# A spare copy with a drain on VectorE, 15 times in each half of a lookup, gram and MLP kernel

## The reference

```python
e = jnp.stack([tbl_f[ids[:, f]] for f in range(27)], axis=1)      # 2048 x 27 x 128
x = jnp.einsum('bfd,bgd->bfg', e, e).reshape(B, 27 * 27)[:, TRIL_IDX]
h = jnp.concatenate([r_bottom_mlp_out, x, r_bottom_mlp_out], axis=1)
h = jnp.maximum(h @ W_top1 + b_top1, 0.0)       # 607 -> 512
h = jnp.maximum(h @ W_top2 + b_top2, 0.0)       # 512 -> 256
y = h @ W_top3                                  # 256 -> 1
```

## Time and profile before

| what | value |
|---|---|
| timed runs, median of 3 | 412.73 us (412.5 to 413.49) |
| profiled execution, span from the first to the last instruction | 563.8 us |
| the profiled execution's own time | not recorded apart from its span |
| TensorE matmul, busy | 395.0 us (70%), 3669 instructions |
| VectorE, busy | 231.8 us (41%), 430 |
| ScalarE, busy | 156.7 us (28%), 337 |
| GpSimd, busy | 292.0 us (52%), 284 |
| mean granted TensorE clock | 0.845 |
| DMA traffic | 40.50 MB, mean 72 GB/s |

### The profile page before, as it was taken

How to read it: one execution, slowest core, us unless ns; L and a number is a source line. 1 busy time by engine, 2 the same in 40 slices (tenths; PEclk the granted TensorE clock), 3 DMA queues, 4 the chain that set the end, 5 groups by cost and what they waited for, 6 DMA issues and landing times.

```text
span 563.8 us, 9147 instructions
## 1 busy us (share of the span) xinstructions
PE 395.0 (70%) x3669; PEld 336.8 (60%) x3669; DVE 231.8 (41%) x430; ACT 156.7 (28%) x337; POOL 292.0 (52%) x284
## 2 busy tenths in 40 slices
PE   1620868397979578688939587797979490924987
PEld 1520756285868467576737376676857390823977
DVE  3530667073836143373617052472716050422430
ACT  3200543021424142324115042322215041401433
POOL 6776007656574747374735737373746656172010
PEclk9975898688989979699969879697979785885999
DMA  8761272122331312041411212140413111030000
GB/s 212 193 170 47 79 185 70 48 84 66 93 86 29 99 35 74 23 118 34 145 28 62 76 33 72 24 117 24 131 37 75 48 53 51 6 95 19 16 8 9
DMA packets 20737, 40.50 MB, mean 72 GB/s; under 512 B 7128, under 2 KB 11428, under 8 KB 20696
## 3 DMA queue, kind: packets, MB, share of 16 engines
q1 hardware_dynamic: 11674, 21.64, 14.1%
q0 software_dynamic: 8960, 18.22, 12.8%
q10 hardware_dynamic: 62, 0.06, 0.1%
HBM read 36.81 MB, written 0.01 MB: 65 GB/s over the span
## 4 chain that ended last, share of the span: by engine, by line
PE 51%; issue 18%; another core or an unknown queue 11%; DVE 8%; DVEq 3%; ACT 3%; DMA 3%; SPq 1%; ACTq 0%
PE col_bank L687 17%; PE gram_bank L723 15%; PE mlp_bank L778 6%; PE mlp_bank L746 6%; DVE mask L583 4%; PE col_bank L706 4%; DVEq L590 3%; PE mlp_bank L742 2%; DMA b<-in_b 2%; DVE mask L587 2%; ACT eT L438 1%; DMA pairs<-in_tbl 1%; DVE parts L624 1%; DVE eT L608 1%
## 5 line engine op out<-in xcount | busy, mean ns | idle before, releaser
L311 POOL DMA_INDIRECT rows<-in_tbl,idx x272 | 285.5, 1050 | 219.2 <-PE gram_bank L723 138.1
L687 PE MATMUL col_bank<-mask,parts 125*128 125x512 f32 (+3 forms) x768 | 168.0, 381 | 21.8 <-DVE parts L624 12.2
L687 PEld LDWEIGHTS col_bank<-mask,parts 125*128 125x128 f32 x768 | 139.8, 204 | 45.0 <-DVE parts L624 12.1
L583 DVE TENSOR_SCALAR mask<-hot_i,rowid 125x1024 fp32r<-125x1024 int32 (+3 forms) x152 | 103.9, 684 | 65.0 <-remote 30.6
L723 PE MATMUL gram_bank<-eT 128*58 128x52 f32 x2048 | 87.2, 244 | 59.6 <-issue 54.0
L723 PEld LDWEIGHTS gram_bank<-eT 128*58 128x58 f32 x2048 | 78.5, 160 | 71.3 <-issue 67.1
L618 DVE COPY pairs<-gram_bank 26x208 f32<-26x208 f32 x128 | 46.7, 365 | 159.4 <-remote 91.5
L706 PE MATMUL col_bank<-ident,rows 128*128 128x128 f32 x272 | 41.7, 293 | 82.5 <-issue 30.5
L468 ACT ACTIVATE pairs<-gram_bank 26x208 f32<-26x208 f32 x128 | 44.5, 348 | 153.0 <-remote 84.6
L706 PEld LDWEIGHTS col_bank<-ident,rows 128*128 128x128 f32 x272 | 32.4, 149 | 90.7 <-issue 88.4
L424 ACT ACTIVATE eH<-col_bank 128x512 f32<-128x512 f32 (+3 forms) x30 | 15.3, 516 | 148.4 <-issue 59.6
(11 more groups left out here) (34 smaller groups left out, 83.9 us busy)
## 6 DMA issues: line engine op xcount, KB each, us to landing
hot_i<-in_hot_ids SPq DMA_DIRECT2D x13, 512.0 KB
rows<-in_tbl,idx POOLq DMA_INDIRECT x272
pairs<-in_tbl SPq DMA_DIRECT2D x8, 448.0 KB
hot_i<-in_hot_ids SPq DMA_DIRECT2D x8, 256.0 KB
pairs<-in_tbl SPq DMA_DIRECT2D x2, 560.0 KB
bottom<-in_bottom SPq DMA_DIRECT2D x8, 128.0 KB
hot_i<-in_hot_ids SPq DMA_DIRECT2D x2, 384.0 KB
x<-pairs SPq DMA_DIRECT2D x16, 39.0 KB
```

Of the source, the lines that this page charges most:

```text
L311: pool.indirect_dma_start(out=rows_of(h, g)[:, i * D:(i + 1) * D], out_offset=None, in_=tables[GATHERED_TABLES[f]], in_offset=bass.Indirec ...
L583: last = nc.vector.tensor_scalar(mask[0:ROWS, entry % MASKS, 0:2 * size], ids, row_of(ks[0], c), None, ALU.is_equal)
L687: last = nc.tensor.matmul(col_bank[fill % BANKS][:, 0:size], parts[k][0:ROWS, part, c * D:(c + 1) * D], mask[0:ROWS, entry % MASKS, at:at ...
```

## The change

A buffer `spare` of 128 x 400 words is added. In each half from 1 to 15 VectorE copies 400 words of the weights `w2` into it and drains, five times ahead of its copies of transposes, ten times ahead of its gram copies. Nothing reads `spare`. The weights have been waited for ahead of the loop.

```diff
+        spare = sb("spare", [128, 400], fp32)
...
+            def refresh_spare(times):
+
+                for _ in range(times):
+                    nc.vector.tensor_copy(spare[:, :], w2[:, 0:2, :].rearrange("p c n -> p (c n)")[:, 0:400])
+                    dve.drain()
+
             for h in range(1, HALVES):
+                refresh_spare(5)
                 for g in groups_of(h):
                     copy_transposed(h, g)
+                refresh_spare(10)
                 copy_pairs(h)
                 if h < LAST:
                     masks_behind_gram(h)
```

## The result

The changed kernel takes 426.16 us (425.28 to 427.44, 4 runs) against 412.62 us (411.54 to 413.49): a ratio of 1.0327, with a 95% interval of 1.0301 to 1.0353. The span of its profiled execution is 424.5 us, and the device time of that execution 426.27 us, so nothing stretches it.

A forecast was written before the change was run, and what follows sets the result against it. GpSimd's gathers bound it, 412.7 us against 400.6 for TensorE and VectorE; the copies bring these to 420.3 and 422.1, and 2 more for halves waiting on the later chain give 424 us, 8 in 10 from 413.5 to 441.

The forecast's parts named there:

- Sum: 412.7: Kernel before, start to end along GpSimd's gathers: 412.7 us, taken as the chain that bounds it.
- 400.6: Kernel before, start to end along TensorE and VectorE: 400.6 us, 12 us under the gathers' chain.
- One copy, 0.50: Each added VectorE copy: 0.45 us and its drain, 0.50 together; 2.5 and 5.0 us a half, 112 us in all.
- The five, even halves: 1.9 and 2.5: Copies ahead of even halves' transposes: TensorE's last six start 1.9 us late, or 2.5 after a half with 52 lookup matmuls.
- The five, odd halves: 0.2 and 0.8: Copies ahead of odd halves' transposes: mostly hidden by layer 1; 0.2 us remain, 0.8 after a half with 52 matmuls.
- The ten: 0.3 in halves 1 and 3 of a cycle: Copies ahead of gram copies: masks 0.3 us late in two of each four halves, 1.3 us at the end.
- The gathers: 6.3: Gathers beside copies lose 0.1 us each, 4.5 a half: 6.3 us in 14 halves, 1.3 more at the end.
- I add 2: On the whole forecast: 2 us more, since each half waits for the later of two chains ending within 2 us.
- Rival 1: Whole kernel: VectorE and TensorE are the bound already, the added cost arrives whole, 436 us; chance 0.20.
- rival 2: Gathers beside copies: each loses 0.5 us through the shared ports, 31 us in all, 445 us; chance 0.08.
- rival 3: Every half: copies fit into VectorE's waits if slack is over 2.5 us; 413 us, no change; chance 0.11.
- the 151 us: Profile before: its 563.8 us span exceeds the 412.73 median by this, taken as a burden of the profiled execution.

The follow-up runs named there:

- e2: The kernel before with the last gather of 17 left out in halves 2 to 15: 395.27 us, ratio 0.9549.
- e3: The changed kernel with only the five copies ahead of the transposes' copies, without the ten: 423.92 us, ratio 1.0231.
- e11: The changed kernel with the five copies left out in even halves, the ten kept in all: 414.97 us, ratio 1.0036.
- e4: The changed kernel with only the ten copies ahead of the gram copies, without the five: 415.78 us, ratio 1.0036.
- e1: The kernel before, unchanged, run for a second profile: 414.69 us, span 412.8.
- e9: The changed kernel with the last gather left out in halves 2 to 15: 428.10 us beside 412.82 for the kernel before, ratio 1.0372.
- e10: The changed kernel with each copy replaced by a sum over 210 words into one word: 418.24 us beside 413.06 for the kernel before, ratio 1.0103.
- e6: The changed kernel with each copy replaced by a sum over 210 words, in the chip 13 series: 562.65 us beside 561.13 for the kernel before.

## Why the prediction was right, point by point

The forecast was 424 us; 426.2 came out, and the mechanism is in the main the forecast one: before, the gathers bound the kernel (e2); the copies fill VectorE's chain beyond them; the five in even halves are the costly ones (e3, e11); the ten nearly hide (e4). Terms of the sums were off, both ways: the base of the chain 5.3 us too high, the cost 11.2 too low, and 2 us added for nothing. That they nearly cancel is luck. I take the periods from gram to gram of e2 and of the changed kernel, since neither is bound by gathers.

- **"Sum: 412.7" by the gathers.** The bound is right. Its front (62.3) was taken from the stretched execution.
- **"400.6" by TensorE and VectorE.** 395.3 at most (e2). The front is 57.6 in e2 in place of 62.3, and half 5 to 6 takes 23.6 in place of 25.4, a period that goes into the sum three times. Cover by the gathers: some 18 us, where I had 12.
- **One copy, 0.50.** Five took 2.1 to 2.45, ten 4.3 to 5.2: right, with 0.416 for the copy itself (I had 0.45).
- **The five, even halves: 1.9 and 2.5.** From the first transposes of half 4 to layer 1 it is 4.25 us in e2 (132.39 to 136.64) and 6.08 after (140.20 to 146.28): 1.83; halves 8 and 12 have 1.9 and 2.0. Behind a half with 52 lookup matmuls (half 6) it is 4.39 against 6.76: 2.37; halves 10 and 14 have 3.2 and 3.3, half 2 has 0.8. In all 15.4 us, where my terms give 15.1. The sum is right, the single halves are not all: in 10 and 14 the last six transposes are slow already (1.32 and 1.51 us, where e2 has 0.84 and 0.85).
- **The five, odd halves: 0.2 and 0.8.** 0 to 0.1 and 0.4 a half, 1.5 us in all where I had 3.0. Half 1 is another matter: no layer 1 stands ahead of its transposes, and from the first of them to the gram it is 4.85 us in e2 (66.10 to 70.95) and 8.17 after (66.08 to 74.25). I left these 3.3 us out, and what follows them: gram 1 takes 3.6 us in e2 and 6.1 after.

```profile
74.25 4.29 PE L732 MATMUL gram_bank<-eT 128*58 128x52 f32 x96 [0.64 <-DVE eT L609]
79.37 1.06 PE L732 MATMUL gram_bank<-eT 128*58 128x52 f32 x32 [0.83 <-DVE pairs L619]
```

The granted clock was 0.62 from 74.2 to 78.6 us (in e2 it was 1.00 in this gram), and the fourth set waited 0.83 us for VectorE: 2.6 us more, 1.5 of them by slow matmuls (4.29 us for 96, where e2 takes 2.77 for as many in gram 0).

- **The ten: 0.3 in halves 1 and 3 of a cycle.** From the start of a gram of an odd half (3 to 13) to the next lookup it is 3.9 to 4.25 us in place of 3.55: 0.3 to 0.7, 3.0 in all where I had 2.1. It is TensorE's fourth set that waits for VectorE's copies, where I had said that it hardly waits. The forecast start of the gram copies, 1 us late, is there: in half 3 ScalarE's start at 130.02, VectorE's at 131.02. From gram 14 to the end nothing is added, where I had 1.3.
- **The clock: not in the sum.** This is the step that failed. I priced a wait of TensorE at its own length. Behind waits among the transposes of even halves (the longest 1.4 to 4.3 us) the granted clock fell, and the first block of layer 1, 1.83 us long, takes 2.4 to 3.3: 7.8 us over the seven halves after, 0.8 in e2, so 7.0 of the change, and 1.5 more in gram 1. The kernel before loses 6.2 us in e1 as well, of which the 1.6 of half 14, behind its last wait for rows, are on its path; the rest lies in the main under its waits for gathers. The row was at hand: 5.3 us of layer 1 in half 5 to 6 (252.34 to 257.68, against 3.7 in half 3 to 4) went into my period of 25.4 as if it belonged there.
- **The whole of it:** 424.5 - 391.8 = 32.7 us between the spans of the changed kernel and e2, all of it behind the first transposes of half 1: 7.0 by the clock in layer 1, 3.3 in half 1 and 2.6 in gram 1, which I had at nothing; the other 19.8 (15.4, 1.5 and 3.0 above, but for rounding) by the terms that I had at 21.5.
- **"The gathers: 6.3" and "I add 2".** Nothing of either. The mean gather went from 1.064 (e1) to 1.076, and e9 shows that no gather's time counts any more. The 4.5 gathers that I let start in 7.5 us should have been 5.5 at one in 1.355 us.
- **"The span after will again be far above the timed runs."** It was 1.8 us below its own run's time.

Rival 1 (VectorE and TensorE the bound already) fell with e2; rival 2 as I put it, GpSimd blocked by copies, fell with e9 and the gathers' 1.076, but the port has a price the other way round: VectorE's wait for GpSimd, and what hangs on it, is worth 8 us (e10), inside my 0.50 a copy; rival 3 fell with e2, where a half's slack is about 18.2 / 14 = 1.3 us and not over 2.5. My reading that the 151 us were a burden of the profiled execution was most likely wrong, though the way out, building from whole pieces, held. What makes TensorE stand for 10 to 20 us on some occasions stays open.

## What to carry to other kernels

When a profile is far longer than the timed runs, sum each engine's uninterrupted chain before trusting its waits: the engine that "waited 138 us" was the bound. Added work is free up to the slack of its own place, not of the engine: with the gathers' slack of some 18 us over them, the 40 copies ahead of the transposes of odd halves cost nothing, the 35 of even halves, where VectorE had little or no gap, 10 us and more. And price a new wait of TensorE with the slower matmuls behind it, here 0.5 to 1.4 us in the first block of layer 1 for each even half.

## What the runs showed of the hardware that I had not expected

- A short wait can cost twice: behind transposes with waits of 0.84, 0.66 and 1.43 us among them the granted clock was 0.54 for 3.3 us (half 4 of the changed kernel); in e3, with the same waits in half 4, it stayed at 1.00. It doesn't fall each time.
- Copies inside SBUF beside gathers: VectorE's copies stretched from 0.369 (median) to as much as 0.620 and 0.416 on the mean; the mean gather of all went from 1.064 to 1.076.
- The same kernel took 412.6 to 413.4 us in four series and 561 in the one on chip 13, TensorE standing inside grams and between transposes. In that series a kernel with VectorE's added work (the sums of e6) was at 562.65, no more than the kernel before, whose runs there spread from 537 to 572.
